# Expert attention: one turn per tile, four fp32r output products, routing weights applied behind them

## The reference, cut to what matters

```python
rw = _gating(n1.reshape(b * t, c), smha_sim, smha_gates, MIN_ATT).reshape(b, t, -1)   # 8 weights a row
q = jnp.einsum('btc,ech,bte->bth', n1, q_proj, rw)      # k and v alike, h = 128
scores = jnp.where(causal, jnp.einsum('bth,bsh->bts', q, k) * scale, -jnp.inf)
attn = jnp.einsum('bts,bsh->bth', jax.nn.softmax(scores, axis=-1), v)
attn_out = jnp.einsum('bth,ehc,bte->btc', attn, o_proj, rw)
hs = x + attn_out
```

## Time and profile before

| what | value |
|---|---|
| median of 3 runs | 1335.94 us (1332.99 to 1341.29) |
| the profiled execution | 1335.94 us, span of its instructions 1334.2 us |
| PE busy | 1179.0 us (88%) |
| DVE busy | 859.9 us (64%) |
| ACT busy | 556.7 us (42%) |
| POOL busy | 314.4 us (24%) |
| mean granted TensorE clock | 0.931 |

### The profile page before, as it was taken

One profiled execution on the slowest core, in us unless ns is written; L12 is line 12 of the kernel. 1 busy time (PEld: TensorE's weight loads), 2 busy tenths in 40 slices (PEclk: granted clock), 3 DMA queues, 4 the chain that ended last, 5 costly groups with the idle time before them and its releaser, 6 DMA issues. The chain is left out here.

```text
span 1334.2 us, 19863 instructions
## 1 busy us (share of the span) xinstructions
PE 1179.0 (88%) x7060; PEld 834.8 (63%) x7060; DVE 859.9 (64%) x1830; ACT 556.7 (42%) x1209; POOL 314.4 (24%) x490
## 2 busy tenths in 40 slices
PE   7789899888878899999788777999989788899999
PEld 3444333333333348777466666999977677788988
DVE  5486777877645758556679676756544455855555
ACT  6215666665646545355235453010023333543332
POOL 5012222222220037344247452000010112400000
PEclk9889999999979769899899787999999889999999
DMA  6850373330624510000030000000030000000000
GB/s 205 175 127 1 56 63 49 49 49 13 106 30 95 103 44 17 0 0 1 0 126 1 1 1 1 1 0 1 1 126 0 1 0 1 1 1 17 16 17 16
DMA packets 38000, 50.69 MB, mean 38 GB/s; under 512 B 11130, under 2 KB 28816, under 8 KB 37264
## 3 DMA queue, kind: packets, MB, share of 16 engines
q1 hardware_dynamic: 37904, 49.44, 17.9%
HBM read 37.26 MB, written 11.77 MB: 37 GB/s over the span
## 5 line engine op out<-in xcount | busy, mean ns | idle before, releaser
L581 PE MATMUL PS<-ARENA 128*17 128x512 f32 (+19 forms) x2208 | 399.4, 429 | 66.0 <-ACT ARENA L1441 16.1
L581 PEld LDWEIGHTS PS<-ARENA 128*17 128x17 f32 (+6 forms) x2208 | 161.6, 125 | 233.6 <-issue 131.4
L1353 ACT ACTIVATE ARENA<-PS 128x512 f32<-128x512 f32 (+3 forms) x384 | 169.9, 495 | 136.6 <-PE PS L581 134.3
L1751 DVE TENSOR_REDUCE ARENA<-PS 128x1 f32<-128x128 f32 (+7 forms) x256 | 182.9, 751 | 46.2 <-PE PS L581 44.4
L581 PE MATMUL PS<-WQKVP,TRR 128*128 128x384 f32 x512 | 133.3, 342 | 1.6 <-ACT BC L1280 1.0
L2196 POOL TENSOR_SCALAR_AFFINE_SELECT ARENA<-ARENA 128x128 f32<-128x128 f32 x256 | 74.4, 300 | 225.9 <-ACT ARENA L1353 224.0
L581 PEld LDWEIGHTS PS<-W2P,INT 128*128 128x128 f32 x768 | 95.1, 188 | 2.9
L581 PE MATMUL PS<-W2P,INT 128*128 128x256 f32 x768 | 95.5, 279 | 0.0
L581 PE MATMUL PS<-TRR,W1P 128*128 128x512 f32 x256 | 88.4, 406 | 7.1 <-ACT BC L1280 7.1
L581 PEld LDWEIGHTS PS<-WQKVP,TRR 128*128 128x128 f32 x512 | 92.5, 190 | 2.8 <-ACT BC L1280 1.9
L2036 DVE SCALAR_TENSOR_TENSOR ARENA<-PS,rw,ARENA 128x384 f32<-128x384 f32 x112 | 69.2, 618 | 38.0 <-PE PS L581 37.1
(11 more groups left out here) (223 smaller groups left out, 1978.5 us busy)
## 6 DMA issues: line engine op xcount, KB each, us to landing
ARENA<-qk_parts SPq DMA_DIRECT2D x96, 128.0 KB, 5.6
ARENA<-xq_parts SPq DMA_DIRECT2D x48, 128.0 KB, 5.8
qk_parts<-ARENA SPq DMA_DIRECT2D x6, 768.0 KB, 3.3
ARENA<-in_w SPq DMA_DIRECT2D x2, 2048.0 KB, 10.7
xq_parts<-ARENA SPq DMA_DIRECT2D x8, 384.0 KB, 2.3
ARENA<-in_wqkv SPq DMA_DIRECT2D x1, 3072.0 KB, 10.2
X<-in_x SPq DMA_DIRECT2D x4, 512.0 KB, 8.6
ARENA<-in_wf SPq DMA_DIRECT2D x2, 1024.0 KB, 7.5
```

Source lines behind the costliest of these rows:

```text
L581: return nc.tensor.matmul(o, lhsT, rhs, start=start, stop=stop, **kw)
L1353: ins = nc.scalar.activation(PROB[GRP * (step % 2) + j][:, 0:w], PS[:, uses[key][0], 0:w], ACT.Exp, scale=HD ** -0.5)
L1751: ins = v.tensor_reduce(negm[:, n % 2, TPB * j + st:TPB * j + st + 1], PS[:, bank:bank + 2, :].rearrange("p b s -> p (b s)")[:, 0:P * (st ...
```

## The change

It does five things. (1) DVE no longer writes eight weighed copies: it writes one, `ATN`, the attention divided by its row sum. (2) PE turns this one block (`at`, now in bank 4, behind `p1`), and ACT and DVE make of it two fp32r parts, `ATP[t % 2][0]` and `[1]`. (3) `o1` becomes four products of 512 columns (two experts each), each in three fp32r terms, in banks 5, 6 and 7 in rotation. (4) DVE applies the routing weights behind them: eight instructions for each tile, each adding 256 weighed columns to `H`, and each waiting for the one before. (5) The output weights are split beforehand into parts: four copies on ACT at tiles 8 to 11 of the `qkv` stage, four subtractions on POOL.

```diff
@@ PE
-            loaded(pe, "wo")
+            pe.wait_ge(wo_split, 4)
...
-                if 0 < i <= TILES:
-                    t = i - 1
-                    drained(pe, ("a1", t))
-                    claim(("at", t), [5, 6])
-                    for e in range(EXPERTS):
-                        ins = nc.tensor.transpose(PS[:, 5 + e // 4, P * (e % 4):P * (e % 4) + P], ATT[:, e, :], ident[:, :])
-                    filled(ins, ("at", t))
                 if i < TILES:
...
                     filled(ins, ("p1", i))
+                if 0 < i <= TILES:
+                    t = i - 1
+                    drained(pe, ("a1", t))
+                    claim(("at", t), [4])
+                    filled(nc.tensor.transpose(PS[:, 4, 0:P], ATN, ident[:, :]), ("at", t))
                 if i > 1:
                     t = i - 2
                     drained(pe, ("at", t))
-                    claim(("o1", t), [7])
-                    for e in range(EXPERTS):
-                        ins = mm(PS[:, 7, 0:D], ATTT[:, e // 4, P * (e % 4):P * (e % 4) + P], WO[:, e, :], start=e == 0, stop=e == EXPERTS - 1)
-                    filled(ins, ("o1", t))
+                    for k in range(4):
+                        bank = 5 + (4 * t + k) % 3
+                        claim(("o1", t, k), [bank])
+                        filled(mm3(PS[:, bank, :], lambda w, _: ATP[t % 2][w], lambda w, _: WOP[w][k], 1), ("o1", t, k))
@@ ACT
+                if 8 <= i < 12:
+                    loaded(act, "wo")
+                    normalized(act, "n1", TILES - 1)
+                    nc.scalar.copy(WOP[0][i - 8], WOC[i - 8]).then_inc(wo_upper, 1)
...
-                    if t >= 1:
-                        arrived(act, ("o1", t - 1))
-                    released(nc.scalar.copy(ATTT, PS[:, 5:7, :]), ("at", t))
+                    if t >= 2:
+                        arrived(act, ("o1", t - 2, 3))
+                    nc.scalar.copy(ATP[t % 2][0], PS[:, 4, 0:P]).then_inc(attn_upper, 1)
@@ DVE
-                    full = [P, EXPERTS, HA]
-                    released(v.scalar_tensor_tensor(out=ATT, in0=PS[:, 4, 0:HA].unsqueeze(1).broadcast_to(full), scalar=s[:, 2:3],
-                                                    in1=rw[:, 0, t, :].unsqueeze(2).broadcast_to(full), op0=ALU.mult, op1=ALU.mult), ("a1", t))
+                    released(v.tensor_scalar(ATN, PS[:, 4, 0:HA], s[:, 2:3], None, ALU.mult), ("a1", t))
                 if i + 1 < TILES:
                     row_max(i + 1)
                 gate_input(1, i, 8, 4)
+                if 0 < i <= TILES:
+                    t = i - 1
+                    dve.wait_ge(attn_upper, t + 1)
+                    released(v.tensor_tensor(ATP[t % 2][1], PS[:, 4, 0:P], ATP[t % 2][0].bitcast(F32), ALU.subtract), ("at", t))
                 if 1 < i <= TILES + 1:
                     t = i - 2
-                    key = ("o1", t)
-                    arrived(dve, key)
-                    released(v.tensor_tensor(H[:, t, :], H[:, t, :], PS[:, 7, 0:D], ALU.add), key)
+                    for k in range(4):
+                        key = ("o1", t, k)
+                        bank = uses[key][0]
+                        arrived(dve, key)
+                        if k > 0:
+                            drained(dve, ("o1", t, k - 1))
+                        link(v.scalar_tensor_tensor(out=H[:, t, :], in0=PS[:, bank, 0:D], scalar=rw[:, 0, t, 2 * k:2 * k + 1],
+                                                    in1=H[:, t, :], op0=ALU.mult, op1=ALU.add))
+                        released(v.scalar_tensor_tensor(out=H[:, t, :], in0=PS[:, bank, D:2 * D], scalar=rw[:, 0, t, 2 * k + 1:2 * k + 2],
+                                                        in1=H[:, t, :], op0=ALU.mult, op1=ALU.add), key)
@@ POOL
+            for k in range(4):
+                pool.wait_ge(wo_upper, k + 1)
+                g.tensor_tensor(WOP[1][k], WOC[k], WOP[0][k].bitcast(F32), ALU.subtract).then_inc(wo_split, 1)
```

More of the change, by code:

```diff
@@ L300, in build @@
         W6 = sb("W6", [P, 6 * KC * D], F32)
+        bc_at = nc.sbuf_base
         BC = sb("BC", [P, len(BCAST), D], F32)
@@ L414, in build @@
         WO = region(27600, 2048, "p (e f) -> p e f", e=EXPERTS)
+        WOC = [region(27600 + 2 * D * k, 2 * D) for k in range(4)]
         W1 = region(15312, 4096, "p (k e f) -> p k e f", k=KC, e=EXPERTS)
@@ L429, in build @@
         PT1 = W6[:, 2048:3072].rearrange("p (t s) -> p t s", t=TPB)
-        ATT = BC[:, 6:10, :].rearrange("p n f -> p (n f)").rearrange("p (e f) -> p e f", e=EXPERTS)
-        ATTT = TR[:, :, N - 4 * P:N]
+        ATN = region(15104, HA)
+        ATP = [[nc.alloc_sbuf_tensor_at(f"ATP{u}{w}", [P, P], F32R, offset=tr_at + 4 * (N - P * (4 - 2 * u - w)))[:, :]
+                for w in range(2)] for u in range(2)]
+        WOP = [[nc.alloc_sbuf_tensor_at(f"WOP0{k}", [P, 2 * D], F32R,
+                                        offset=bc_at + 4 * D * (6 + 2 * k) if k < 3 else arena_at + 4 * 14336)[:, :] for k in range(4)],
+               [part(f"WOP1{k}", 27600 + 2 * D * k, 2 * D, "p (e f) -> p (e f)", e=2) for k in range(4)]]
         RANK = tmp[:, :, :].rearrange("p u (i e j) -> p u i e j", i=4, e=EXPERTS)
@@ L502, in build @@
         wqkv_split = sem("wqkv_split")
+        wo_upper = sem("wo_upper")
+        wo_split = sem("wo_split")
+        attn_upper = sem("attn_upper")
         w1_split = sem("w1_split")
@@ L2049, in second_norm @@
                 if c is not None:
-                    drained(dve, ("o1", 4 * c + 3))
+                    drained(dve, ("o1", 4 * c + 3, 3))
                     statistics(H, batches[c])
```

## The result

| | before | changed |
|---|---|---|
| median, 20 runs each | 1333.88 us | 1340.05 us |
| ratio, 95% interval | 1 | 1.0058 (1.0032 to 1.0084) |
| profiled execution, span | 1334.2 us | 1332.9 us |
| first to last reciprocal of the row attention | 136.7 us | 138.2 us |
| last reciprocal to the first subtraction of the feed-forward (the tail) | 22.9 us | 27.8 us |

The changed kernel is 0.6% slower: the ratio with its interval stands for some 7.7 us, the two medians alone for 6.2. The spans of two single executions can't show that: they differ by as much in stages that the change leaves alone. The two stretches of the row attention can: together they grew from 159.6 to 166.0 us, 6.4 us.

What follows compares the result with a forecast made beforehand. PE was taken to set the pace of the row attention, busy 134.7 of 158 us. Span 1334.2 - 2.0 (first stretch) + 2.0 (tail) + 2.0 (clock) = 1336.2 us, plus 1.7 around it: 1338 us, range 1317 to 1360.

Steps and rivals of the forecast that it cites:

- The forecast (C): Whole kernel: the chain takes what PE saves; within 1% of before, 1325 to 1349 us; chance 0.53, within 1% 0.50.
- The chain: Row attention, reciprocal to next reciprocal: maximum, exponential, copy, subtraction, eight additions in line; turns sum to 134.7 us against 136.7.
- PE's saving: PE's turns and `o1` in the row attention: 1.5 us a tile, 24 us in all, which turn into PE's waiting.
- PE's own path: PE's fourth product, V, scores and probabilities in a turn: mostly ends before the chain; 7.6 us for s = 4.
- The first stretch: First to last reciprocal of the row attention: 134.7 us against 136.7 before, a gain of 2.0; turn 13 at 20.6 us.
- The additions: Eight weighed additions of 256 columns on DVE: 0.516 us each, 4.13 us a tile, bounds 0.41 and 0.6 us.
- The tail: Last reciprocal to the feed-forward's first subtraction: 24.9 us taken from 21 to 27, against 22.9 before, 2 us lost.
- The clock: Row attention: PE relapsing to 1.2 GHz behind two pauses a tile; 2 us added for one or two relapses.
- Rival (A): Row attention: both pauses make PE fall to 1.2 GHz in every tile; 17 us slower, 1355 us; chance 0.27.
- Rival (B): Waiting for the forerunner costs nothing, additions at 0.41 us: 13 us less, 4 more by full clock; 1321 us, chance 0.20.
- Things at nothing: ACT's four copies and POOL's four subtractions in `qkv` are hidden, no DMA added, feed-forward untouched: no cost.
- The busy times: Sign in the row attention after the change: DVE's busy time near 125 us, PE's below 115.

Runs made afterwards that it cites:

- e1: Changed kernel with ACT's copy of the turned block ahead of the exponential of tile i + 1; ratio to the kernel before 0.9952.
- e4: Changed kernel with PE turning the one block eight times into the same place instead of once; ratio to the kernel before 1.0064.
- e2: Changed kernel without the even expert's weighed addition of each pair, so half the additions; ratio to the kernel before 0.9836.
- e3: Changed kernel with unread bf16 products filling PE's pauses from turn 4 on and before the gate in turns 8 and 12; ratio to the kernel before 1.0022.
- e10: Changed kernel with POOL's splitting of the feed-forward's weights done earlier; ratio to the kernel before 1.0026.
- e9: Changed kernel with even and odd experts' additions in two sums, joined by one more addition; ratio to the kernel before 0.9995.

## Why the prediction was right, and where it was off

The forecast was 1338 us with a range of 1317 to 1360; measured are 1340.05 us, and the difference to before lies within 1%, the case given 0.50. The forecast (C) is the one that the runs bear out: the mechanism was right. That the number came so close is in part luck. The forecast added 0 to the two stretches and 2 us for the clock, and measured are 6.4 us; but it started from three runs with a median of 1335.94 us, and twenty give 1333.88, so a start 2 us too high hid half of the miss.

- **The chain.** Maximum, exponential, copy, subtraction, additions: shown by the turn after and by e1, which loosens one link. Turns 3 to 8 took 7.0, 7.3, 9.7, 9.4, 7.6, 7.5 us where 7.0, 7.3, 9.5, 9.5, 7.7, 7.6 stood.
- **PE's saving is worth little here.** Shown by e4: spent again, 13 us of PE's work cost 3 us, or 4.5 without turns 1 and 2.
- **PE's own path** was summed up wrongly. The terms as written add up to 8.1 us for s = 4 (8.3 with s + 1), not to 7.6 (8.2), more than the chain's 7.3 of turn 4. The turn after bears this out: the fourth product starts 4.06 us behind the reciprocal and the next `at` 4.14 us behind that, without a wait, while the turn took 7.25 us. PE's path is right behind the chain in turns 3 and 4, and e2 gained little there (1.1 and 0.7 us).
- **The first stretch** was mis-sized by 3.5 us: 138.2 for 134.7. 1.35 of it is turn 13 (21.95 for 20.6 us), 1.2 turns 1 and 2 (PE at the low clock; e3 and e10 took 11.3 us there where 12.3 stood), 1.2 turns 9, 14 and 15. A gain of 2 became a loss of 1.5 us.
- **The additions** cost 4.23 us in the view for 4.13: 0.51 within a pair, 0.59 across two. The upper bound of 0.6 us that I had for a hand-over was nearly right for every second one.
- **The tail** was mis-sized by 2.9 us, 27.8 for 24.9, at the upper bound of 21 to 27 and a little above; the terms written for it add up to 20.7 to 25.1, so 24.9 was near their top. The logits ended at 10.3 us, within 9 to 11.4. The weights' instructions took 6.9 us with the last of them (3.5 in turn 13, where POOL is idle), against 5.9 at most in the sum; the additions 4.4 for 4.1; statistics with what follows them 2.8 for 2.0; the centring 3.4 for 1.7. That it takes 3.4 beside POOL stood in the trace of before. e10 shows POOL's part.
- **The clock.** I added 2 us for relapses that reach the path. There were some: 2.2 us in turns 1 and 2 of the profiled execution, and about 0.9 us in the tail, where the logits ran from 1116.30 to 1120.12, half of them at 1.00 and half at 0.50 (2.9 us at full clock before). They are not of the kind that I had in mind, behind the two pauses of each tile, and turn 13 stood in the sum at the low clock already.
- **Rival (A)** falls with the granted clock of the changed kernel and with e3. In turns 3 to 7 and 11 the clock was 1.00, with pauses of up to 1.4 us before the fourth product and of 1.9 us before `at`; turns 4 to 8 and 10 to 12 did not move with PE kept busy. The Trainium skill ("TensorE: Matmul & The Clock Gate", section on psum-queue depth-cycling) tells of a clock that swings for short waits between groups; in these turns this case's trace disagrees. It is not that such a fall can't happen: in turn 7 of e10, behind a pause of 1.9 us as in the changed kernel, the clock fell to 0.80, and the turn took 8.37 us for 7.64. Over the whole stage it did sink, from 0.92 to 0.84: in turns 1, 2, 8 to 10, 13 and 15 and in the tail.
- **Rival (B)** named a real cost: e9 shows the pace of 0.39 us once the link is gone. It was no forecast for the kernel as changed, whose additions are linked.
- **Things at nothing.** In `qkv` POOL's and ACT's new work moved no wait: PE's busy time in a stretch of 67 us (900 to 967) is 67.00 us before and after.
- **The busy times** missed what was named as a sign. With the window moved along with the stage (968 to 1132.4 us) DVE is busy for 119.9 us, not 125, and PE for 123.2, not below 115. For PE the lower clock is a likely reason, since its busy time grows with it; for DVE none was looked for.

## What to carry to other kernels

Taking work from the engine that sets the pace gains only until the next engine's chain is longer; sum up that chain in program order, with every instruction that merely stands ahead in the queue, and take each price from a row in which the same neighbours are busy. When a change closes such a loop, look first at the order on the engine in the middle: two swapped lines turned 0.6% slower into 0.5% faster. And a running sum in one place is a chain of waits: two sums with one joining addition beat it though they need one instruction more. Before a stretch of one execution is held against another's, compare the granted clock of its turns: here it made 2 us in turns that no edit touched.

## What the runs showed of the hardware

- Some DVE instructions are slowed while POOL splits weights, those with two tensors in SBUF and small ones with one: 128 x 32 took 1.25 us instead of 0.17 (L1937 in the changed kernel and in e10), four centrings 3.39 us instead of 1.67. The additions with one operand in PSUM were not: in e10 the weighed ones from 1103.98 to 1108.29 kept 0.47 to 0.48 us beside it, and before, L2085 its 0.42 us.
- An addition of 256 columns out of PSUM shows 0.48 us, but the next independent one starts 0.39 us after it (e9), a linked one 0.51 us, and one that waits at another bank's semaphore 0.59 us (changed kernel, turn 11).
- The clock can fall while PE has no pause. In e10 PE was busy without a gap through the gate's logits, products of 8 columns: up to 1083.65 at a granted clock of 0.98, behind it at 0.50, with 0.57 us instead of 0.36 for two of them. With the filling ahead of them (e3) they ran at 1.00 throughout, and the scores directly behind at 0.53 (3.15 us for 1.67).
